# Image 1's o and x loaded only when the last row's transposing transfers have landed

## The reference, cut to what matters

```python
def _L1_conv_ref(x, ln_w, ln_b, Wq, Wk, Wv, w1, w2):
    ...
    S = jnp.einsum('bnd,bmd->bnm', Q, K)
    attn1 = jax.nn.softmax(S, axis=-1)
    attn2 = jnp.square(jax.nn.relu(S))
    e1, e2 = (jnp.exp(w1), jnp.exp(w2))
    attn = e1 / (e1 + e2) * attn1 + e2 / (e1 + e2) * attn2
    out = jnp.einsum('bnm,bmd->bnd', attn, V)
    ...
x = x + _L0_conv_ref(_gn(x), ...)
x = x + _L1_conv_ref(_gn(x), ...)
```

## Time and profile before

| What | Value |
|---|---|
| time, median of 3 runs | 3390.74 us |
| lowest and highest of them | 3389.33 and 3391.31 us |
| the profiled execution's own time | 3385.89 us |
| its span | 3384.1 us |
| mean granted TensorE clock | 0.972 |
| PE's busy tenths in the 40 slices | 3799999999999999999998978999999788999998 |
| loads of image 1's x, of its o to `vb`, of its o to `neg` | 8, 4 and 4 of 384.0 KB each |

### The profile page before, as it was taken

How to read it: one execution, slowest core, us unless ns; L and a number is a source line. 1 busy time by engine, 2 the same in 40 slices (tenths; PEclk the granted TensorE clock), 3 DMA queues, 4 the chain that set the end, 5 groups by cost and what they waited for, 6 DMA issues and landing times. The chain is left out here.

```text
span 3384.1 us, 47902 instructions
## 1 busy us (share of the span) xinstructions
PE 3196.7 (94%) x16354; PEld 1276.9 (38%) x16354; DVE 1903.8 (56%) x2461; ACT 2205.7 (65%) x2430; POOL 933.8 (28%) x485
## 2 busy tenths in 40 slices
PE   3799999999999999999998978999999788999998
PEld 1222222222223222222222224555555344555555
DVE  6551347431554524376211155888888556888886
ACT  5356556566555665565665634988888257888886
POOL 1002021020020210210200001666666214666665
PEclk8799999999999999999999989999999889999999
DMA  4412112111132021220230013677777834777777
GB/s 125 117 29 62 46 38 69 45 38 51 30 84 52 16 64 44 49 60 25 53 91 21 5 48 86 125 143 143 144 144 144 147 93 99 143 143 144 143 143 136
DMA packets 685380, 286.18 MB, mean 85 GB/s; under 512 B 602416, under 2 KB 644144, under 8 KB 682608
## 3 DMA queue, kind: packets, MB, share of 16 engines
q1 hardware_dynamic: 680656, 275.92, 38.3%
q10 hardware_dynamic: 4544, 8.00, 1.2%
HBM read 85.99 MB, written 34.21 MB: 36 GB/s over the span
## 5 line engine op out<-in xcount | busy, mean ns | idle before, releaser
L495 ACT ACTIVATE prob<-ps_s,cur 128x1024 f32<-128x1024 f32 x1024 | 1085.0, 1110 | 740.0 <-PE ps_s L715 738.9
L728 PE MATMUL ps_a<-prob,vt 128*64 128x512 f32 x4096 | 993.4, 606 | 0.0
L1486 POOL TENSOR_TENSOR p_lo<-gp,p_hi 128x1024 f16<-128x1024 f32 x256 | 550.3, 2160 | 383.6 <-ACT p_hi L1623 378.5
L1766 PE MATMUL ps_s<-kst,qs 128*128 128x512 f16 x2560 | 637.9, 382 | 15.8 <-DVEq L1957 10.6
L1779 PE MATMUL ps_o<-v_hl,at_hi 128*128 128x384 f16 x2048 | 550.0, 330 | 27.2 <-DMA at_lo<-p_lo 25.3
L709 PE MATMUL ps_s<-q_a,k_a 128*128 128x512 f16 x2048 | 535.6, 384 | 5.3 <-DMA q_b<-lo 2.1
L1779 PE MATMUL ps_o<-v_hl,at_lo 128*128 128x192 f16 x2048 | 506.4, 248 | 0.0
L728 PEld LDWEIGHTS ps_a<-prob,vt 128*64 128x64 f32 x4096 | 249.2, 136 | 409.4 <-issue 408.7
L1954 DVE TENSOR_SCALAR_CACHE_REDUCE neg<-ps_s,a_mix 128x1024 f32<-128x1024 f32 x256 | 327.3, 1279 | 114.4 <-PE ps_s L1766 113.3
L709 PEld LDWEIGHTS ps_s<-q_a,k_a 128*128 128x128 f16 x2048 | 133.5, 98 | 542.2 <-ACT prob L495 470.6
L1766 PEld LDWEIGHTS ps_s<-kst,qs 128*128 128x128 f16 x2560 | 244.3, 98 | 241.5 <-issue 14.2
(11 more groups left out here) (229 smaller groups left out, 2727.5 us busy)
## 6 DMA issues: line engine op xcount, KB each, us to landing
z<-z_scratch SPq DMA_DIRECT2D x80, 384.0 KB, 3.7
sq<-rn_scratch SPq DMA_DIRECT2D x14, 768.0 KB, 10.3
qs<-q_scratch SPq DMA_DIRECT2D x64, 128.0 KB, 2.7
rden<-den_scratch SPq DMA_DIRECT2D x64, 96.0 KB, 2.2
o_scratch<-o_s SPq DMA_DIRECT2D x64, 96.0 KB, 2.0
res_scratch<-a_xg SPq DMA_DIRECT2D x4, 1536.0 KB, 7.1
q_scratch<-qst SPq DMA_DIRECT2D x32, 192.0 KB, 2.4
res<-res_scratch SPq DMA_DIRECT2D x64, 96.0 KB, 2.1
```

Of the source, the lines that this page charges most:

```text
L495: act.activation(prob[:, n % PR, :], ps_s[:, n % 2, :], ACT.Exp, bias=cur[:, slot:slot + 1], scale=1.0 / SPLIT).then_inc(exped, 1)
L728: ins = pe.matmul(ps_a[h * HALF:(h + 1) * HALF, j % 2, :], vt[:, slot, m, :], prob[:, a % PR, h * CH:(h + 1) * CH], start=(m == 0), stop=( ...
L1486: pool.tensor_tensor(p_lo[:, cols], prob[s][:, cols], p_hi[:, cols], ALU.subtract).then_inc(lo_made[c], 1)
L1766: ins = pe.matmul(ps_s[:, c % 2, h * CH:(h + 1) * CH], qs[:, s, qt, :], kst[:, ktile, cols], start=(t == 0), stop=(t == len(terms) - 1))
```

## The change

The loads of chunks 0 to 3 leave their places between the squares and high parts of ACT's slot 31. They now stand at that slot's end. Ahead of each chunk's pair of loads ACT waits until both transposing transfers of piece c of row 31 have landed (the count 32 x 32 of `turned[c]` for b = 0). The waits that guarded the first loads (L1639 to L1641) stay where they were, and the loads of chunks 4 to 7 follow as before.

```diff
                             act.wait_ge(s_full, b * USE + USE)
                             for c in range(NQ):
                                 act.wait_ge(p_made[c], RB * (b + 1) - 1)
-                            bring(0, True)
-                            bring(0, False)
                         relu(t + 1, 1 - s, 0)
                         square(t, s, 3)
-                        if last:
-                            bring(1, True)
-                            bring(1, False)
                         square(t, s, 1)
                         exp_piece(t + 1, 1 - s, 0)
                         high(t, s, 0)
-                        if last:
-                            bring(2, True)
-                            bring(2, False)
                         square(t, s, 2)
...
                         relu(t + 1, 1 - s, 3)
                         if last:
-                            bring(3, True)
-                            bring(3, False)
+                            for c in range(NQ):
+                                act.wait_ge(turned[c], 32 * RB * (b + 1))
+                                bring(c, True)
+                                bring(c, False)
                             for c in range(NQ):
                                 act.wait_ge(relued[c], RB * (b + 1))
                                 act.wait_ge(exped[c], RB * (b + 1))
```

## The result

| What | Before | After |
|---|---|---|
| time, median | 3388.74 us | 3394.28 us |
| lowest run | 3385.54 us | 3391.39 us |
| profiled execution's own time | 3385.89 us | 3398.49 us |
| its span | 3384.1 us | 3396.7 us |

A forecast was written before the change was run, and what follows sets the result against it. Prediction: PE bounds the kernel, 94% busy; only a gap between images can move. Chunk 3's projection ends at 2682.1 instead of 2677.2, so +4.9 us on the 3390.74 median: 3395.7, range 3387.5 to 3402.0.

The forecast's parts named there:

- rival (c): ACT's loads: transposing transfers held behind two pairs, each turn 8.5 us or more; +10.4 us, 3401.1; chance 23%.
- What the change removes: Row 30: loads no longer beside pieces 1 to 3, groups 2 to 5 weighed by about 2647, ten us sooner, unusable.
- Rival (d): Row 30's early freeing on PE pays, only if chunk 0 lands before 2654.3; faster; chance 5%.
- The first load: ACT's slot 31: row 31's piece 0 has landed and chunk 0's pair is issued at 2650.0 us.
- The turns: ACT's waits between the pairs of chunks 0 to 3: 8, 7 and 7 us, with `turned[3]` at 2672.
- A pair's time: Chunk loads on ACT's queue: 6.4 us from a pair's issue to its landing, when alone.
- The clock: PE's projections after idling: a start at half clock costs 2 us, before chunk 0 and again before chunk 2.
- What follows chunk 3: After chunk 3's projection: unchanged work, chunks 4 to 7 landing in time with 5 us of cover.
- The rival of the loads keeping up: ACT's loads: `turned[2]` and `turned[3]` come between pairs, PE runs without gaps; -4.7 to +1 us, 3388.7; chance 14%.
- the shares of one crowded window: DMA engines, 2645 to 2650 us: ACT's loads moved 0.91 MB, SP's transposing transfers 0.18 MB; used for the turns.

The follow-up runs named there:

- the last version: All eight pairs of loads on SP's queue, chunks 4 and 5 behind row 31's piece 1, 6 and 7 behind piece 2: 0.9980 of the kernel before.
- chunk 0 early: Changed kernel without its waits on row 31, chunk 0's pair back at its old place, chunks 1 to 3 at the slot's end: 1.0009 of the kernel before.

## Why the prediction was right

The forecast was +4.9 us and 3395.7; measured was +6.1 (3.7 to 8.5) and a median of 3394.28. The place of the loss and its mechanism were right. Three terms of the sum had the wrong size. In the first profile, with the 1.3 us of its lateness taken off, the first load came 0.6 us later than forecast, the turns took 2.6 more, chunk 3's pair 1.2 less (5.2 for 6.4), and its projection ended 2.6 later after that landing, for the clock: 4.5 us in all. So this passage lost 9.3 us where the forecast had 4.9, close to rival (c)'s 10.4, and the five profiles together say 7.9. The time's 6.1 lies nearer to the forecast than to (c), but its interval allows 7.9 as well: that the number came out so near is in part luck. So is the nearness of 3395.7: its base, a median of 3 runs (3390.74), is 2.0 above that of 20.

- **What the change removes.** Right. Row 30's transfers land in 3.1 to 3.4 us again, and groups 2 to 5 of row 30 were done at 2648.6 us (2647.3 without the 1.3 by which this execution was late; 2647 was forecast). None of it is a gain with the waits in, as forecast. Without them it is 3.7 us, and with all loads on SP's queue 6.8. Rival (d) had named this condition, an earlier chunk 0: it came at 2652.3 in the last version, 1.1 of that lateness in the execution.
- **The first load.** Forecast 2650.0, measured 2651.89, or 2650.6 in the forecast's time. Right.
- **The turns.** Forecast 8, 7 and 7 us, measured 9.3, 3.0 and 12.3 in the first profile and 8.2, 3.0, 14.1 and 9.6, 2.9, 13.9 in the others. The sum was forecast at 22 and was 24.6, 25.3 and 26.4. Here the step failed that spread pieces 2 and 3 evenly over the turns: piece 2's low part was issued just ahead of chunk 1's pair and slipped through in 3.93 us, so chunk 2's pair was issued 3.0 us behind chunk 1's, and piece 3 then met two pairs at once. That is rival (c)'s mechanism ("held behind two pairs"), paid for in part by the early second turn. Its sign came true as well: `turned[3]` after 2673.9, where it came at 2675.1, 2675.9 and 2676.9 in the three profiles, each in the first passage's time.
- **A pair's time.** Taken as 6.4 from a pair nearly alone. Chunk 0's o landed 8.1 us after its own issue, beside both parts of piece 1 and the high part of piece 2. Chunk 2's took 13.5 beside chunk 1's pair and piece 3. I had put the sharing on the transposing transfers only; it goes both ways. Chunk 3's, alone, took 4.8.
- **The clock.** I took 2 us for a start at half clock from the earlier trace rows (the 16 matmuls from 2657.30 took 4.02 us, at a granted clock of 0.50 until 2661) and let chunk 3's wait hide the second one. Measured: 3.0 for chunk 0 (6.64 less 3.67), and 2.8 for chunks 2 and 3 (9.83 less 7.03), not hidden in the first and third profile, because chunk 3 had landed by the time it was wanted (2676.80 plus 4.8, 2681.6; chunk 2's projection would have ended at 2681.7 at the full clock).
- **What follows chunk 3.** Right: from chunk 3's residual to row 31's output copy it took 24.7 us before and after (2677.34 to 2702.02, 2687.99 to 2712.67), and PE waited for none of the chunks 4 to 7.
- **The rival of the loads keeping up** needs `turned[2]` and `turned[3]` between pairs. It got the first and not the second, in all three profiles.
- **How many pairs a transfer meets.** Row 31's piece 3 (low part) landed in 3.2 us with no pair beside it, in 9.5 to 10.1 with one and in 13.4 to 15.3 with two. The forecast had the shares of one crowded window; what decides how the DMA engines divide between two queues, no run here shows. Those shares say nothing of which transfer will meet which pair, and there most of the forecast's error in the turns lay.

## What to carry to other kernels

A wait that keeps a load clear of one transfer can push it into the next (here the late loads let row 30's transfers land in 3.1 to 3.4 us, and row 31's piece 3 took 13.4 to 15.3): ask of each load what it will run beside at its new time, and what will wait for that. Where two queues share the DMA engines and somebody waits for the transfers of one, try the loads on that same queue, in the order in which all are needed, before adding waits between them: that was the fastest version here (0.9980), and the one with only half of the loads moved gained nothing (0.9999). And compare stretches of several profiles, not two spans: here the spans differed by 12.6 us and the times by 6, and the unchanged rest of the program varied by 5.

## What the runs showed of the hardware

- Between two groups of loads on one queue, with none in flight, row 31's piece 1 landed in 3.4 us (all chunks on SP's queue); beside chunks on ACT's queue the same piece took 17.2 us (chunks 0 to 3 on SP's queue) and 22.5 us (chunk 0 early).
- The issue of a transposing transfer on SP's queue grew too: 1.2 to 1.4 us with no loads about, 5.70 in the changed kernel, 10.59 in the second profile of the kernel before (row 31's piece 3, beside chunks 4 to 7). In each of these two the transfer was issued while loads were in flight; why its issue takes longer then, no run shows.
- PE's clock: chunk 0's projection, after idle stretches of 9.7 to 19.4 us, took 6.0 to 7.0 us instead of 3.67, and began at a granted clock of 0.50. So did work after some shorter ones: 6.94 us after 2.48 us of idle (chunks 0 to 3 on SP's queue), 9.83 for two projections after 3.16 (changed kernel). Where chunk 2 waits for piece 3, chunk 1's projection took 5.37 us after 2.53 us of idle (first profile), but it began at 1.00 and fell to 0.50 by 2674. After 2.14 us in the changed kernel a projection ran at 1.00 throughout. What sets the clock, these runs don't show.
